# Attention on one core: one maxima item ahead of each stretch, and at most eight key tiles to a visit

## What is computed

```
q = x @ wq (32 heads of 32), k = x @ wk, v = x @ wv (8 heads of 32, each serving 4 query heads)
attn = softmax(causal(q k^T / sqrt(32)));  x = layernorm(x + (attn v) @ wo)
x = layernorm(x + ffn(x))       ffn: x @ weight.T + top-2-of-8 gated LoRA of rank 16
```

## Time and profile before

| | |
|---|---|
| median of 3 runs | 3619.89 us (3619.73 to 3621.58) |
| profiled execution, its own time | 3618.96 us |
| its span, first to last instruction | 3617.1 us |
| mean granted TensorE clock | 0.987 of 2.4 GHz |
| busy: PE, DVE, ACT, POOL | 97%, 53%, 41%, 43% of the span |
| attention | from about 563 to 2680 us, 16 groups |
| a steady group, from one step 2 to the next | 130.08 us |

### The profile page before, as it was taken

The page is one execution under the profiler, slowest core; times in us unless marked ns, Lnnn a source line. Parts: engine busy times, 40 slices in busy tenths (PEclk is TensorE's granted clock), DMA queues, the critical chain, the costliest instruction groups (busy, mean ns, idle before and its releaser), DMA issues. The chain is left out here.

```text
span 3617.1 us, 63262 instructions
## 1 busy us (share of the span) xinstructions
PE 3496.1 (97%) x26058; PEld 2441.7 (68%) x26058; DVE 1920.7 (53%) x3577; ACT 1493.0 (41%) x1839; POOL 1560.4 (43%) x672
## 2 busy tenths in 40 slices
PE   8999998999999999999999999999969999999999
PEld 7888885555565565565565556556537888888887
DVE  3121217666666666666666666666615666642223
ACT  3111112555555555555555555555542222221111
POOL 0000002867867877787786787787530000000000
PEclk9999997999999999999999999999989999999999
DMA  6343325021111111111111111110026787755553
GB/s 209 117 129 114 110 87 116 23 51 48 34 41 48 44 30 50 47 31 49 48 30 50 48 35 38 48 38 9 12 84 203 230 226 225 214 192 173 177 182 128
DMA packets 248224, 340.69 MB, mean 94 GB/s; under 512 B 55440, under 2 KB 150288, under 8 KB 247952
## 3 DMA queue, kind: packets, MB, share of 16 engines
q1 hardware_dynamic: 247952, 336.87, 31.6%
HBM read 203.08 MB, written 133.17 MB: 93 GB/s over the span
## 5 line engine op out<-in xcount | busy, mean ns | idle before, releaser
L680 DVE TENSOR_REDUCE p_part_max<-p_qm 128x1 f32<-128x512 f32 (+3 forms) x2240 | 1351.6, 667 | 711.0 <-PE p_qm L533 448.7
L503 POOL TENSOR_TENSOR p_psums<-p_psums,p_probs 128x1024 f32<-128x1024 f32 x560 | 1331.9, 2378 | 82.1 <-ACT p_probs L643 2.2
L643 ACT ACTIVATE p_probs<-p_km 128x1024 f32<-128x1024 f32 x896 | 902.9, 1023 | 445.2 <-PE p_km L561 384.2
L533 PE MATMUL p_qm<-p_k_st,p_q_st 96*128 96x512 f32 (+3 forms) x2560 | 911.9, 425 | 14.7 <-DMA p_q_st<-q_hi 10.8
L533 PEld LDWEIGHTS p_qm<-p_k_st,p_q_st 96*128 96x128 f32 x2560 | 483.9, 195 | 244.7 <-DVE p_part_max L680 170.0
L561 PE MATMUL p_km<-p_q_st,p_k_st 97*128 97x512 f32 x1792 | 609.8, 422 | 5.1 <-ACT p_probs L643 5.1
L568 PE MATMUL p_o<-p_probs,p_v 128*32 128x256 f32 (+1 forms) x9216 | 581.3, 371 | 0.0
L499 POOL TENSOR_TENSOR p_psums<-p_probs 128x1024 f32<-128x1024 f32 x95 | 226.4, 2383 | 489.2 <-ACT p_probs L643 489.2
L568 PEld LDWEIGHTS p_o<-p_probs,p_v 128*32 128x32 f32 x9216 | 270.8, 110 | 214.5 <-issue 61.9
L561 PEld LDWEIGHTS p_km<-p_q_st,p_k_st 97*128 97x128 f32 x1792 | 304.0, 190 | 143.8 <-issue 104.2
L41 PE MATMUL p_acc<-p_xT_hi,p_w_hi 128*128 128x512 f32 x640 | 250.2, 391 | 9.6 <-DVE p_w_lo L226 9.6
(11 more groups left out here) (150 smaller groups left out, 4130.1 us busy)
## 6 DMA issues: line engine op xcount, KB each, us to landing
p_q_st<-q_hi SPq DMA_DIRECT2D x128, 256.0 KB, 4.8
p_x_raw<-in_xT SPq DMA_DIRECT2D x64, 256.0 KB, 3.4
q_hi<-p_out_hi SPq DMA_DIRECT2D x64, 256.0 KB, 2.0
q_lo<-p_out_lo SPq DMA_DIRECT2D x64, 256.0 KB, 2.3
p_q_st<-q_lo SPq DMA_DIRECT2D x64, 256.0 KB, 4.4
attended_T<-p_o_raw SPq DMA_DIRECT2D x128, 128.0 KB
p_a_raw<-attended_T SPq DMA_DIRECT2D x32, 512.0 KB, 5.3
p_recip<-reciprocals SPq DMA_DIRECT2D x128, 128.0 KB, 6.9
```

Of the source, the lines that this page charges most:

```text
L503: pool.tensor_tensor(sums[:, :, :], sums[:, :, :], probs[s % PB][:, :, :], ALU.add).then_inc(added, 1)
L533: last = pe.matmul(bank[:, x * keys:(x + 1) * keys], q_st[par][0:ROWS, c, h + x, sub * P:(sub + 1) * P], k_st[par][0:ROWS, j * CK:j * CK + ...
L643: act.activation(tile[:, :, :].rearrange("p h q -> p (h q)"), km[s % 2][:, :, :].rearrange("p a b -> p (a b)"), ACT.Exp, scale=SCALE).then ...
L680: dve.reduce_max(part_max[c][:, h:h + heads, sub, j], qm[bank_of(i)][:, 0:item_width(i)].rearrange("p (h k) -> p h k", h=heads), AX.X).the ...
```

## The change

Three edits. `MOST` goes from 5 to 8, so the slots hold 2, 4, 6, 8, 5, 5, 6, 6, 7, 7, 8, 8 steps: 12 stretches and 12 visits to a group. The ring `probs` goes from 18 to 22 buffers, and as 72 is no multiple of 22 its index now counts on over the groups. And the first item of a stretch's first step is issued ahead of that step's scores on TensorE; the order of the items among themselves stays, and so does the order on the other engines.

More of the change, by code:

```diff
@@ L498, in group @@
                             at_least(pool, chunk_done, n * NCHUNK + max(0, plan.chunks[c] - 1))
-                            pool.tensor_tensor(sums[:, :, :], probs[(s - 1) % PB][:, :, :], probs[s % PB][:, :, :],
+                            pool.tensor_tensor(sums[:, :, :], probs[(n * NS + s - 1) % PB][:, :, :], probs[(n * NS + s) % PB][:, :, :],
                                                ALU.add).then_inc(added, 1)
@@ L502, in group @@
                             pool.wait_ge(added, n * NADD + plan.adds_through(s) - 1)
-                            pool.tensor_tensor(sums[:, :, :], sums[:, :, :], probs[s % PB][:, :, :],
+                            pool.tensor_tensor(sums[:, :, :], sums[:, :, :], probs[(n * NS + s) % PB][:, :, :],
                                                ALU.add).then_inc(added, 1)
@@ L581, in values @@
                     t = STEPS[s][1]
-                    last = weighted(v[par][:, t, :], probs[s % PB], 0, offset(s), t == 0)
+                    last = weighted(v[par][:, t, :], probs[(n * NS + s) % PB], 0, offset(s), t == 0)
                     if not plan.on_pool(s):
-                        last = weighted(ones[:, :], probs[s % PB], CQ, offset(s), False)
+                        last = weighted(ones[:, :], probs[(n * NS + s) % PB], CQ, offset(s), False)
                 last.then_inc(slot_done, 1)
@@ L635, in exps @@
                 c, t = STEPS[s]
-                tile = probs[s % PB]
+                tile = probs[(n * NS + s) % PB]
                 if t >= 2 * c:
```

## The result

The changed kernel takes 3613.81 us (median of 20 runs, 3603.49 to 3627.37) where the kernel before takes 3619.81: ratio 0.998, 95% interval 0.9974 to 0.9986. That is 6.0 us less. The forecast was 3605; the time lies in the range (3588 to 3621), but the gain is 6 us where 15 were forecast. It also scatters more: 24 us between its fastest and slowest run, 13 for the kernel before.

The account below looks back on a forecast made before the run. DVE was taken to bound stretches and POOL's adds each group from step 42. Fourteen groups at -1.32 us gave -18.5, group 0 -2, group 15 0; with the clock's +5.8, -14.7: 3605 us median, range 3588 to 3621.

Parts of the forecast that it names:

- The line of 1.197 us a step with its negative constant: Stretches inside a group: DVE bounds them, k steps taking 1.197 k - 0.215 us, as three full banks cover the visit.
- the two parts of a group: Steps 2 to 41 take 71.4 us, where savings count; from step 42 on 58.7 us, which PE savings cannot shorten.
- POOL's 55 us as the floor of the second: From step 42 on, POOL's 22 adds without idling, 55.2 us, set the time to the next step 2.
- a moved visit, fewer visits, -1.26: Ahead of step 42: three visits fewer save 0.39 us; two pooled steps moved behind it save 0.87 us a group.
- a shrinking wait at POOL: Sign at the group's end: the 1.64 us wait should grow to about 1.9; shrinking would mean POOL was no bound.
- Group 15's second half has no items and is bound by ACT; there merging helps: Last group: merging helps, its first half loses the moved visit's profit; together 0 us (-1 to +1).
- a longer wait at POOL: Ends of groups: it makes clock drops more frequent, 7 of 14 waits instead of three, +5.8 us.
- The item ahead: Stretch starts: 0.25 us less where unmerged and DVE-bound; steps 2 to 5 pay 0.25, POOL starts 0.24 us later.
- The low bound of 3588: Whole kernel: no ACT wait or later POOL start, -1.9 us a group, three clock drops, -3 in group 0.
- A: Rival, all visits: PE alone bounds, each of 96 saved visits gives 0.41 us; -39 us, 3580; chance 0.12.
- B: Rival, waits at POOL: the clock falls after every one, 10 us above forecast, 3615, no distinguishable change; chance 0.15.
- D: Rival, steps 2 to 5: low clock holds throughout, +4.8 us after every longer wait, about 3662, slower; chance 0.08.

Follow-up runs that it names:

- experiment 3: The changed kernel with POOL adding 12 instead of 13 tiles of chunk 7 (groups 0 to 14): 3583.93 us, ratio 0.9897.
- Experiment 11: The kernel before with POOL adding 12 instead of 13 tiles of chunk 7, nothing else: 3595.2 us, ratio 0.9933.
- experiment 4: The changed kernel without the item ahead of a stretch's first scores: 3613.18 us, ratio 0.9985 to the kernel before.
- experiment 8: The changed kernel with step 35's maxrow item behind the visit, 12 tiles for POOL, long slots and added matmuls in group 15: 3557.19 us, ratio 0.9824.
- 6: The changed kernel with group 15 in slots of at most five, step 35's maxrow item behind the visit, 12 tiles of chunk 7 for POOL: 3555.62 us.
- Experiment 7: The changed kernel with two unused matmuls of 512 columns after each step's scores in group 15, from step 36 on: 3603.91 us, ratio 0.9962.
- experiment 1: The changed kernel with group 15 alone cut into slots of at most five again: 3600.89 us, ratio 0.9948.
- experiment 2: The changed kernel with the maxrow item of step 35 issued behind the visit that follows: 3579.74 us, ratio 0.9882.
- 8 to 11: Includes two runs on the kernel of 6: with added matmuls in group 15 (9), 3559.28 us; without the item ahead (10), 3557.47 us.

## Why the prediction was wrong

**Right: what bounds a steady group.** The line of 1.197 us a step with its negative constant, the two parts of a group, and POOL's 55 us as the floor of the second were confirmed by the stretch of 5.53 us, by 1.55 us less ahead of step 42, by 128.8 us for the group, and from the other side by experiments 3 and 11. The cover lost by a merge shows by itself in experiment 4, which has no item ahead: steps 12 to 19 take 9.75 us in one stretch, 4.96 + 4.56 = 9.52 in two. The 9.12 us of steps 56 to 63 confirm nothing, as they are 9.09 without the item ahead; two stretches took 4.31 + 4.97 = 9.28 there, one with a maxrow item. The step "a moved visit, fewer visits, -1.26" (1.25 in the profile) carries nearly the whole gain: without the item ahead the group is as short. The prediction named a shrinking wait at POOL as a sign that POOL was no bound, and the wait did shrink, from 1.64 to 1.52 us. The sign was badly chosen: the adds have no gap, and taking one away shortens the group in both kernels.

**The first step that failed: "Group 15's second half has no items and is bound by ACT; there merging helps ... 0 (-1 to +1)".** The term was to be 0 and measured +9.4 us (+9.7 to the program's end). The sum gave 3604.3 us for the profiled execution, which took 3616.9: of the 12.6 us missing there, this term is three quarters. It failed twice.
- *The sign of merging.* "There merging helps" was stated without a sum. The kernel before takes 4.5 us for five such steps and 3.5 for four: 1.03 us a step less about 0.6 for a stretch, since the last exps of each run beside the visit. A negative constant is lost with every merge, as I had written for DVE's three banks and did not carry over to ACT's two `km` buffers. The stretches of the kernel before from step 42 on add up to 26.5 us, those of the changed kernel to 29.3. Where the clock stays up, the long slots cost 3.3 us (experiment 8 against 6) to 4.4 us (7 against 1); these are single profiles, and the long side has the added matmuls too.
- *The clock.* In a long stretch without items PE waits on ACT up to five times in a row, 0.17 to 0.73 us each, and the granted clock fell; the visit that follows, which PE could have done at full pace, then took up to 1.6 times as long (4.97 us for 3.16). Experiment 7 keeps the slots and adds work, and the visits get 7.6 us shorter, group 15 7.0; experiment 1 cuts the slots, no low clock is left, and group 15 gets 11.4 us shorter. Four profiles with long slots and no added matmuls (the changed kernel, experiments 2 to 4) have 17 to 24 us of low clock in group 15; the six with slots of at most five have 0 to 7. With either repair the time (3603.9, 3600.9 us) is below the 3605 of the forecast.

**The second: the place of the drops in the steady groups.** I took 7, and there were 7 in the profiled execution (an eighth, at 664 us, is group 0's); but I gave the cause as a longer wait at POOL. That wait became 1.52 us, not 1.9, because the stretches behind step 42, which I had 0.5 us shorter, took as long as before (37.1 us in both) and PE came later. Only two of the seven drops stood behind it. The other five stood behind the row maximum of step 35, which the prediction did not price: merging put it at the end of a stretch, the wait grew from 1.15 to 1.35 us, and a visit in 32-column groups comes right behind it. That more of DVE's work is then outstanding is argued; no run isolates it. In the kernel before none of these 16 waits was followed by a drop. A number that comes out right for the wrong place is luck. Nor does one kind of wait explain it: experiment 3 keeps all the waits for row maxima and has one drop, experiment 2 keeps those for POOL alone and has as much low clock as six, experiment 4 keeps both and has its seven mostly behind POOL. In the kernels without a wait at POOL (3, 6, 8 to 11) the steady groups have one drop or none. What decides whether a given wait is followed by a drop stays open; nothing here was made to tell it.

**Smaller terms.** The item ahead was reckoned to give 0.25 us in a plain stretch and to cost in POOL's start and in steps 2 to 5. The size of the gain was right (5.53 for 5.76 us in steps 20 to 24), its place only in part (nothing in steps 56 to 63 and 64 to 71, losses in 6 to 11 and behind step 42 that had no term); steps 2 to 5 lost 0.05 instead of 0.25; the sum over the group is nothing at eight steps, 0.36 us at five and 0.2 us once POOL doesn't bind. Up to the first mark 2.7 us were gained where group 0 (2, 0 to 3) and the first steady group (1.3) were to give 3.3, with a drop at 664 us that the kernel before had not. The low bound of 3588 lies 2 us below its own terms (3619.9 - 14 x 1.9 - 3 = 3590), and the top of the range, 3621, is not the high bound that was worked out, 3625.

Of the rivals, A (each visit worth its whole switching, 39 us) is out: the group lost 1.2 us, not 6 x 0.41 = 2.5. The Trainium skill (TensorEngine Tiling, Key Properties) says that changing the tiling mode drains TensorE. The gaps of 0.10 to 0.18 us at the ends of a visit agree with it, and every visit still pays them; only 0.13 us of the 0.41 came back per visit saved, since the rest ran beside DVE. B and D are out: of the 14 waits at POOL two were followed by drops. But the mechanism on which they stood, the clock as the price of idling, took more than half of what is missing (7.0 us in group 15 of 12.6), at places they didn't name. In every profile of this case waits of 0.2 to 1.95 us were followed by drops. The Trainium skill (TensorE: Matmul & The Clock Gate, "Why this matters for your kernels") asks for no idle gap over about 3 us between matmul bursts; here, keeping to that was no protection.

## What to carry to other kernels

Where two engines share a ring of buffers, read the law of a stretch as (pace) x (steps) - (cover): merging stretches loses one cover each (0.23 us in steps 12 to 19), and so the fixed price of a switch comes back only in part. Before pricing an edit inside a loop, find which part of the period another engine's chain fixes (here POOL's 55 us); time saved beside that chain becomes waiting, and one add a group taken off it was worth 25 us, four times the edit. And price the part of the program in which the filler work is missing by itself: where the matmul engine idles in small pieces, the clock may fall, and then it is the dense work behind the gaps that pays.

## What was not expected of the hardware

- The granted clock fell to 1.2 GHz after single waits of 1.35 us (five times in the steady groups of the changed kernel's profile), and after rows of waits of 0.17 to 0.73 us with matmuls between them (24 us in its group 15). A drop in its steady groups costs 1.4 us of 128.8 behind the wait at POOL, mostly 1.6 behind step 35.
- Giving TensorE 72 useless matmuls of 512 columns beside its waits made group 15 7.0 us shorter in the profile (the medians differ by 9.9 us, with fewer drops elsewhere).
- Twenty executions of the changed kernel spread by 24 us, and the clock goes with it: the fastest (3603.5) has a mean granted clock of 0.986, the slowest (3627.4) 0.978. Experiment 11, without a wait at POOL, spread by under 4 us in five executions (3593.5 to 3597.4).
